# A new order table for a two-layer adaLN kernel on one core: TensorE's signals held back inside groups of indirect transfers

## The reference

```python
h = layernorm(x) * (1 + ca) + sa
x = x + ga * L0_attn(h)    # 16 heads of 8, rope on q and k, softmax over 512 keys
h = layernorm(x) * (1 + cb) + sb
x = x + gb * L0_ffn(h)     # 8 experts, top 2 of each token, silu(h @ w0) * (h @ w1) @ wo
...
h = layernorm(x) * (1 + ca) + sa
x = x + ga * L1_attn(h)    # v, gate = silu(h @ W_hidden); q, k from silu(h @ W_qk)
                           # sim = q.T @ k (256 x 256); out = v * sum(softmax(sim)) * gate @ W_out
h = layernorm(x) * (1 + cb) + sb
x = x + gb * L1_ffn(h)     # expert of a batch: gelu(h @ w1 + b1) @ w2 + b2
```

## Time and profile before

| | before |
|---|---|
| median of 3 runs | 965.92 us (959.76 to 969.08) |
| the profiled execution's own time | 969.92 us |
| its span on the core | 967.7 us |
| mean granted TensorE clock | 0.929 |

### The profile page before, as it was taken

How to read it: one execution, slowest core, us unless ns; L and a number is a source line. 1 busy time by engine, 2 the same in 40 slices (tenths; PEclk the granted TensorE clock), 3 DMA queues, 4 the chain that set the end, 5 groups by cost and what they waited for, 6 DMA issues and landing times. The chain is left out here.

```text
span 967.7 us, 15545 instructions
## 1 busy us (share of the span) xinstructions
PE 803.7 (83%) x4976; PEld 442.4 (46%) x4976; DVE 707.5 (73%) x1415; ACT 576.3 (60%) x907; POOL 469.6 (49%) x609
## 2 busy tenths in 40 slices
PE   4366776899889888999989999988998898688676
PEld 2111122345345534654455545654664466365354
DVE  6688578779878778867778888767686736567664
ACT  2245574757677667765777587567755854433332
POOL 4143125203567546782767376457557653862201
PEclk9669699899999999999899999999999999799787
DMA  6435044353655342295245355552337053110000
GB/s 179 147 106 132 33 81 156 105 116 104 219 139 148 118 137 72 75 273 152 67 110 179 122 156 126 173 172 76 89 102 232 15 176 123 58 38 20 1 23 27
DMA packets 101306, 110.65 MB, mean 114 GB/s; under 512 B 16409, under 2 KB 81049, under 8 KB 99882
## 3 DMA queue, kind: packets, MB, share of 16 engines
q1 hardware_dynamic: 97082, 102.06, 37.3%
q0 software_dynamic: 3584, 7.35, 2.3%
q10 hardware_dynamic: 560, 0.26, 0.1%
HBM read 82.98 MB, written 26.26 MB: 113 GB/s over the span
## 5 line engine op out<-in xcount | busy, mean ns | idle before, releaser
L1754 DVE TENSOR_REDUCE negmax<-scores_for_max 128x2 f32<-128x1024 f32 x252 | 307.6, 1221 | 80.8 <-PE scores_for_max L1050 73.7
L1453 ACT ACTIVATE probs<-scores 128x1024 f32<-128x1024 f32 x256 | 261.7, 1022 | 107.4 <-PE scores L1074 93.5
L1084 PE MATMUL weighted_values<-probs,vaug 128*32 128x512 f32 x1024 | 142.9, 636 | 0.0
L1050 PE MATMUL scores_for_max<-ks,qs 48*128 48x512 bf16 x504 | 103.3, 406 | 42.0 <-DVE negmax L1754 37.0
L1146 PE MATMUL expert_units<-xt,ring 128*128 128x128 f32 x840 | 119.8, 284 | 9.3 <-DVE mu L1938 6.1
L1146 PEld LDWEIGHTS expert_units<-xt,ring 128*128 128x128 f32 x840 | 103.2, 191 | 45.4 <-issue 44.6
L1074 PE MATMUL scores<-qs,ks 51*128 51x512 bf16 x512 | 104.3, 404 | 16.8 <-ACT probs L1453 14.6
L1050 PEld LDWEIGHTS scores_for_max<-ks,qs 48*128 48x128 bf16 x504 | 24.7, 94 | 126.8 <-DVE negmax L1754 96.7
L2217 POOL DMA_INDIRECT xs_d<-xbn,rowpos x56 | 55.0, 983 | 45.0 <-DVE rowpos L1887 30.1
L2228 POOL DMA_INDIRECT y<-ys_d,rowpos x56 | 55.4, 989 | 29.8 <-issue 15.7
L1199 PE MATMUL shared_ab<-ring,mu 128*128 128x128 f32 x420 | 57.8, 283 | 2.5 <-ACT slot_rows L1579 1.1
(11 more groups left out here) (329 smaller groups left out, 1572.0 us busy)
## 6 DMA issues: line engine op xcount, KB each, us to landing
ring<-in_experts SPq DMA_DIRECT2D x113, 384.0 KB, 5.0
slot_rows<-xs_d SPq DMA_DIRECT2D x7, 960.0 KB
parts_d<-parts SPq DMA_DIRECT2D x15, 384.0 KB, 2.7
qs<-parts_d SPq DMA_DIRECT2D x14, 384.0 KB, 6.2
ks<-parts_d SPq DMA_DIRECT2D x14, 384.0 KB, 9.7
ys_d<-slot_rows SPq DMA_DIRECT2D x21, 256.0 KB
w<-in_L_ffn_w SPq DMA_DIRECT2D x16, 256.0 KB, 4.1
parts_d<-parts SPq DMA_DIRECT2D x15, 256.0 KB, 2.9
```

The lines of the kernel that those rows point to most:

```text
L1050: last = nc.tensor.matmul(max_bank(b, g, n)[:, 512 * m:512 * (m + 1)], qs[at, b % 2, p, t * P:(t + 1) * P], ks[at, b % 2, p, :], start=Tru ...
L1084: last = nc.tensor.matmul(pv[32 * j:32 * j + 32, :], vaug[:, kt, PAIRS * (j // 2) + GP * g + j % 2, :], probs[:, kt % 2, j % 2, j // 2, :] ...
L1453: nc.scalar.activation(probs[:, kt % 2, j, :, :].rearrange("p m s -> p (m s)"), se[:, :], ACT.Exp)\
L1754: V.tensor_reduce(negmax[:, g % 2, :, n], max_bank(b, g, n)[:, :].rearrange("p (m s) -> p m s", m=2), AX, ALU.max, negate=True)\
```

## The change

Only `SLOTS` is new. Each step is still done, once, by the same instructions on the same engine, with the same DMAs; what is new is the order on each engine, and with it which user of a shared PSUM bank waits for which. Many steps are empty for some batches (`ldown`, `row` and `upb` do something for batch 7 alone), and their numbers move too, without an effect. Of the steps that do something, 597 of 1231 stand at another place on TensorE, 295 of 688 on ScalarE, 328 of 753 on VectorE, 95 of 301 on GpSimd and 55 of 184 on SyncE. Up to about 157 us the orders are practically the same, and up to about 475 us they differ little. The search went on from the old order; in its picture of the chip TensorE's signals (its semaphore updates) are now held back while GpSimd is inside a group of indirect transfers.

Some lines of the diff:

```diff
-        ("C", "upb"): dict(pe=(1, 2, 3, 4, 5, 6, 7, 11, 12, 13, 14, 15, 16, 17, 1372, 1373)),
+        ("C", "upb"): dict(pe=(1, 2, 4, 12, 16, 17, 18, 20, 21, 22, 23, 24, 25, 26, 1372, 1375)),
...
-        ("C", "row"): dict(pe=(53, 54, 55, 57, 58, 59, 60, 1350)),
+        ("C", "row"): dict(pe=(38, 39, 40, 41, 42, 43, 44, 1347)),
...
-        ("A", "mT"): dict(pe=(157, 179, 200, 221, 244, 268, 298, 312, 339, 382, 402, 436, 460, 508, 544, 560, 607,
-        634, 668, 732, 778, 803, 844, 888, 924, 950, 993, 1050, 1081, 1133, 1177, 1217)),
+        ("A", "mT"): dict(pe=(157, 179, 200, 221, 244, 268, 298, 312, 339, 382, 402, 439, 461, 509, 544, 560, 607,
+        634, 668, 732, 778, 811, 865, 895, 926, 958, 998, 1048, 1085, 1128, 1175, 1200)),
...
-        ("C", "qk"): dict(pe=(534, 546, 687, 698, 840, 852, 992, 1025, 1130, 1139, 1242, 1259, 1325, 1329, 1358,
-        1359)),
-        ("C", "hid"): dict(pe=(556, 562, 581, 586, 713, 719, 734, 740, 867, 873, 891, 896, 1039, 1055, 1060, 1063,
-        1161, 1169, 1185, 1189, 1266, 1269, 1280, 1283, 1341, 1343, 1344, 1346, 1355, 1356, 1360, 1361), act=(249,
...
+        ("C", "qk"): dict(pe=(534, 546, 687, 698, 824, 834, 980, 1017, 1138, 1146, 1241, 1258, 1325, 1330, 1360,
+        1362)),
+        ("C", "hid"): dict(pe=(556, 562, 581, 586, 713, 719, 734, 740, 846, 852, 870, 877, 1029, 1043, 1050, 1057,
+        1171, 1177, 1190, 1193, 1264, 1266, 1279, 1282, 1335, 1344, 1346, 1348, 1355, 1356, 1358, 1359), act=(249,
...
-        ("C", "w2g"): dict(pool=(34, 169, 201, 249, 271, 310, 342, 351)),
+        ("C", "w2g"): dict(pool=(34, 167, 196, 248, 271, 310, 338, 351)),
...
-        ("C", "rstd3"): dict(pool=(129, 170, 213, 257, 298, 312, 347, 352)),
+        ("C", "rstd3"): dict(pool=(129, 170, 204, 250, 298, 312, 347, 352)),
```

More of the change, by code:

```diff
@@ new lines @@
+        ("B", "y"): dict(pe=(261, 388, 523, 659, 844, 963, 1109, 1262)),
+        ("B", "xT"): dict(pe=(275, 413, 549, 686, 869, 1001, 1142, 1281)),
+        ("B", "gate"): dict(pe=(281, 416, 554, 689, 876, 1003, 1145, 1304)),
+        ("B", "rank"): dict(pe=(289, 421, 561, 697, 885, 1007, 1152, 1153)),
+        ("B", "rowT"): dict(pe=(319, 322, 346, 368, 484, 487, 505, 526, 624, 629, 647, 674, 770, 774, 808, 827, 933,
+        937, 956, 977, 1079, 1082, 1099, 1116, 1203, 1206, 1224, 1235, 1236, 1237, 1238, 1239)),
@@ new lines @@
+        ("C", "out"): dict(pe=(594, 595, 746, 747, 886, 888, 1063, 1064, 1197, 1198, 1287, 1288, 1349, 1350, 1373,
+        1374)),
+        ("C", "xT3"): dict(pe=(609, 766, 907, 1074, 1209, 1307, 1351, 1376)),
+        ("C", "up"): dict(pe=(612, 617, 623, 630, 769, 780, 785, 793, 910, 916, 929, 987, 1077, 1084, 1090, 1100,
+        1210, 1215, 1220, 1225, 1309, 1311, 1313, 1314, 1352, 1354, 1357, 1361, 1377, 1378, 1379, 1380), act=(280,
+        285, 288, 294, 370, 378, 383, 391, 450, 456, 462, 498, 542, 548, 555, 564, 616, 621, 626, 632, 676, 678, 680,
@@ L253 @@
-        95, 96, 97, 98, 99, 100, 101, 102, 919, 924, 929, 932, 937, 946, 948, 950)),
-        ("C", "keep"): dict(dve=(45, 46, 47, 103, 104, 105, 106, 958), pool=(113, 151, 193, 236, 266, 305, 337, 341)),
-        ("P", "stats"): dict(dve=(113, 193, 278, 335, 395, 472, 557, 640)),
+        ("P", "split"): dict(act=(35, 38, 44, 53, 62, 76, 121, 131, 190, 206, 279, 317, 363, 384, 483, 495), dve=(181,
+        187, 211, 212, 213, 214, 215, 216, 217, 218, 219, 220, 221, 222, 223, 224), pool=(14, 15, 36, 40, 45, 48, 65,
@@ new lines @@
+        71, 91, 95, 132, 150, 171, 183, 226, 231)),
+        ("P", "split2"): dict(act=(36, 39, 46, 55, 64, 79, 122, 135, 192, 208, 282, 323, 367, 389, 485, 503),
+        dve=(182, 189, 194, 195, 197, 198, 201, 202, 203, 204, 205, 206, 207, 208, 209, 210), pool=(2, 3, 37, 42, 46,
+        51, 67, 73, 92, 100, 133, 153, 173, 185, 228, 234)),
+        ("A", "mrow"): dict(act=(43, 57, 68, 78, 90, 101, 118, 124, 140, 159, 168, 186, 198, 224, 242, 252, 275, 297,
+        315, 354, 377, 401, 426, 442, 460, 478, 504, 527, 549, 576, 595, 607), sp=(61, 63, 66, 68, 70, 74, 77, 80, 82,
@@ new lines @@
+        ("B", "stats"): dict(dve=(332, 399, 472, 554, 651, 728, 807, 885)),
+        ("B", "logits"): dict(dve=(340, 412, 484, 564, 670, 741, 822, 901)),
+        ("B", "top"): dict(dve=(343, 413, 485, 566, 671, 742, 823, 902)),
+        ("B", "place"): dict(dve=(345, 416, 488, 568, 675, 744, 827, 836)),
+        ("B", "weights"): dict(dve=(347, 455, 533, 621, 709, 790, 858, 912)),
+        ("C", "stats"): dict(dve=(456, 536, 622, 712, 794, 860, 913, 949)),
+        ("C", "stats2"): dict(dve=(464, 546, 632, 721, 804, 868, 920, 956)),
@@ new lines @@
+        ("P", "rstd"): dict(pool=(6, 32, 38, 57, 78, 119, 155, 200)),
+        ("A", "vcopy"): dict(pool=(31, 54, 76, 106, 145, 186, 222, 262)),
+        ("C", "w2g"): dict(pool=(34, 167, 196, 248, 271, 310, 338, 351)),
+        ("A", "mparts"): dict(pool=(35, 43, 49, 50, 53, 55, 60, 72, 75, 77, 79, 82, 94, 107, 110, 117, 130, 143, 149,
+        168, 177, 188, 199, 201, 214, 224, 236, 249, 255, 267, 275, 293)),
+        ("B", "rstd"): dict(pool=(56, 80, 114, 152, 198, 233, 266, 309)),
+        ("B", "scatter"): dict(pool=(59, 61, 62, 63, 64, 66, 68, 69, 83, 84, 85, 86, 87, 88, 89, 90, 120, 121, 122,
@@ L323 @@
-        ("B", "fetch"): dict(sp=(75, 76, 85, 89, 92, 95, 106, 109, 112, 115, 126, 132, 134, 138, 149, 153, 158, 161,
-        171, 172, 179, 181, 188, 193, 198, 201, 208, 210, 214, 216, 218, 220)),
+        ("B", "x2"): dict(pool=(108, 144, 184, 223, 261, 301, 331, 332)),
+        ("C", "rstd"): dict(pool=(109, 146, 187, 225, 263, 302, 333, 346)),
+        ("C", "rstd2"): dict(pool=(112, 148, 192, 229, 265, 304, 336, 348)),
+        ("C", "lo"): dict(pool=(116, 154, 194, 235, 269, 306, 340, 341)),
@@ new lines @@
+        ("C", "rstd3"): dict(pool=(129, 170, 204, 250, 298, 312, 347, 352)),
+        ("P", "rope"): dict(sp=(1, 4, 24, 25, 26, 30, 31, 32)),
+        ("P", "second"): dict(sp=(2, 5, 6, 7, 8, 9, 10, 11)),
+        ("P", "raw"): dict(sp=(3, 16, 17, 18, 19, 20, 23, 27)),
+        ("P", "late"): dict(sp=(12, 35, 36, 37, 38, 39, 40, 41)),
+        ("B", "blank"): dict(sp=(13, 14, 21, 22, 28, 29, 33, 34)),
+        ("P", "load"): dict(sp=(15, 43, 58, 72, 84, 103, 124, 155)),
+        ("P", "store"): dict(sp=(42, 44, 62, 64, 67, 69, 79, 81, 98, 100, 119, 130, 142, 145, 168, 175)),
```

255 lines of the change are left out of this document (108 added, 147 removed), and 112 rows, old and new, of the table SLOTS.

## The result

The new order takes 970.4 us in the median of 16 runs (968.59 to 977.91), the old one 966.69 us in 16 runs (959.76 to 973.11). The ratio is 1.0054, with a 95% interval of 1.003 to 1.0078: slower by half a per cent, where 0.25% faster was forecast. The new order's profiled execution took 970.33 us, at its median; that of before took 969.92 us, 3.2 us above the median of its now 16 runs. So the two profiles differ by 0.4 us where the medians differ by 3.7, and single differences between them must be read with that in mind.

The account below looks back on a forecast made before the run. TensorE's own work was taken to bound the middle, chains through VectorE, ScalarE and GpSimd the tail. −2.0 + 1.5 + 0.9 − 1.8 − 1.0 = −2.4 us gave 967.5 profiled, 963.5 us as median; range 951 to 977.

Parts of the forecast that it names:

- middle: 157 to 800 us: same work in another order, few holes to fill; −1 us, ends −8 and +8.
- (a): Around 811 us: hole filled, gate/7 behind out/5, layer 1 of batch 5 and the gathers behind it sooner; −2.0 us.
- (b): Around 879 us: hid0/6, ldown5/7, w07/7 ahead of sim/6, other hid steps behind it, out/6 later; +1.5 us, ends 0 and +3.
- (c): At 920 us: hid1/7 and hid3/7 ahead of qk0/7 and qk1/7, VectorE runs out of work; +0.9 us, ends 0 and +2.
- (d): At 942 us: bias row upb1/7 moves from ahead of out/7 into the hole behind it; −1.8 us.
- The premise: TensorE's signals come late inside groups of indirect transfers; judged unsupported, as the windows' 15.9 us of hole matched their surroundings.
- named risks: In the middle: rstd3/2 waiting ahead of six scatters, up to 5 us; a row DMA behind an expert fetch, some 6 us.
- second risk: In the middle: a row DMA queued behind a fetch of experts, 11 us from mT less 4.6 us cover, some 6 us.
- The first rival: New order fills half of the 15.9 us of holes in the transfer groups: 956.5 us, chance 0.22.
- The second, slower one: Engines stop on steps moved ahead of their data, at rstd3/2 or a row DMA in the middle: 975.5 us, chance 0.23.
- a rule on GpSimd and VectorE against the premise: GpSimd and VectorE lock each other out of a shared port; 2.5 us per meeting by the rule, at most 1.7 traced.

Follow-up runs that it names:

- f2: New order, but the old one between ldown3/7 and xT3/6 (870 to 909 us): 967.0 us against 965.2 before, ratio 1.0011.
- f1: The new order run once more, unchanged: 971.0 us against 965.2 before on the same chip, ratio 1.0066.
- h1: The new order run again, unchanged: 970.9 us against 966.1 before on the same chip, ratio 1.0061.
- f3: New order, but the old one from ldown3/7 to the first pieces of sim/7 (870 to 931 us): 965.3 us against 965.2 before, ratio 1.0003.
- h4: Same kernel as f3, run again: 964.9 us against 966.1 before on the same chip, ratio 1.0004.
- j1: New order, but row/7 behind out/6 on TensorE, lacc7/7 and stats/7 behind hid3/6's step on VectorE: 999.9 us against 1011.4 before, ratio 0.9893.
- e3: Old order, with the new one only behind the first pieces of sim/7: 1002.6 us against 1006.4 before, ratio 0.9965.
- g2: Same kernel as e3, run again on the same chip: 1004.7 us against 1006.2 before, ratio 0.9989.
- j3: Same kernel as e3, run on another chip: 1010.8 us against 1011.4 before, ratio 0.9992.
- e1: Old order, with the new one only between ldown3/7 and xT3/6 (870 to 909 us): 1008.4 us against 1006.4 before, ratio 1.0014.

## Why the prediction was wrong, by its own steps

The forecast was 2.4 us under before, and the new order is 4.8 us over it on open chips (the mean of 3.7, 5.8 and 4.8). Term by term:

| term | forecast | measured | known from |
|---|---|---|---|
| middle | −1.0 | about +1.6 | what the others leave; uncertain by about 3 us |
| (a) | −2.0 | about +0.4 | two profiles |
| (b) | +1.5 | +4.4 (5.2 against the profile of before) | 16 profiles; f2 took back 4.0 |
| (c) | +0.9 | +0.3 | 19 profiles, spread wider than the difference |
| (d) | −1.8 | −1.9 | 19 profiles |

(b) is the largest part of the loss and the one that an experiment shows. It is not the whole miss: with (b) as forecast the kernel would still have been some 2 us slower. (a) won nothing, and the middle may have cost what it was to win. The forecast in absolute time is off by 0.8 us more, because it stood on a median of three runs.

**The premise.** It said that nothing shows a delay that ought to be planned around. For the chip that the profile came from this is right, and two more results on open chips (f1, h1: +0.66 and +0.61%) bear it out. As a statement on the kernel on any chip it is wrong: on two of the four chips of the experiments the delay is there, and the kernel before takes 40 us more there. A profile of one chip could not have told it.

**The middle**, −1 us forecast. The two profiles would give it 4 us of gain (xT/6 at 855.90 against 859.92), but that of before is 3.2 us over its median. Worked out from the loss of 4.8 us on open chips: the stretch at 880 us takes 4.4 of it (52.9 less 48.5, the mean of the eleven old ones), 920 us some 0.3, and the end gives 1.9 back. That leaves 2.0 us for everything ahead of xT/6, of which (a) has some 0.4, with an uncertainty that I put at about 3 us. f3 and h4, which keep only the new middle, (a) and the new end, come out near it: level with before although the end gives 1.9. The sign of this step isn't settled. Its named risks did not happen: rstd3/2 went through between two scatters without a wait, since layer 1 of batch 2 came 17 us sooner, not 12.9. GpSimd's timeline of the new order:

```profile
542.14 0.96 POOL L2217 DMA_INDIRECT xs_d<-xbn,rowpos  x1 [0.30 <-issue]
543.17 0.23 POOL L2102 TENSOR_SCALAR rstd_d<-mv_d 128x4 f32<-128x4 f32 x1
```

TensorE's waits for a row DMA come to 0.2 us. The price of that second risk was read too low: from mT at 156.38 us to `exp` at 169.04 it is 12.7 us and not 11, so that one bad meeting would have been some 8 us.

**(a), −2.0 us forecast, nothing measured.** xT3/5 did come sooner (821.93 us against 828.24, 6.3 us, of which 4.4 were there at the end of sim/5 already), so the 2 us were won on TensorE. The step went wrong in letting the gathers follow. They hang on out/5, which came 4.7 us sooner, 0.3 more than sim/5; the first gather moved from 825.12 to 820.69 and the last piece of x2/6 from 844.53 to 839.66, by 4.4 and 4.9 us, so at most 0.5 more than the shift already there. The up layers reached the same late sum sooner and waited longer: the last hole grew from 3.02 us to 5.63. Behind that hole TensorE was on its lower clock for longer: the 16 matmuls of dn and the 4 behind them take 3.78 and 2.77 us, against 3.49 and 1.88 before. That gave back the half microsecond and more, as xT/6 comes 4.0 us sooner.

```profile
821.93 0.66 PE L1007 MATMUL shared_pc<-ident,xdn 128*128 128x128 f32 x4 [1.86 <-ACT xdn L1437]
...
844.43 1.86 PE L1356 MATMUL shared_pc<-w,kq 128*128 128x128 f32 x7 [5.63 <-DVE kq L2046]
...
820.69 1.07 POOL L2228 DMA_INDIRECT y<-ys_d,rowpos  x1 [0.49 <-issue]
...
839.66 1.29 POOL L682 TENSOR_TENSOR x<-y,x 128x512 f32<-128x512 f32 x1
```

**(b), +1.5 us forecast, 5.2 measured between the two profiles (4.4 against the mean of the old ones): the largest step.** The mechanism and the first half of the sum were right. It put hid2/6 30.6 us behind xT/6; it came 30.9 behind. Wrong was "two steps of 3.07 us" and the 3.7 behind them: 3.5, 4.0 and 4.4 us (together 2.1 us more). I had counted TensorE's work between the steps and put at nothing what that work waits for and the clock. ldown7/7 waits 0.74 us for VectorE's product, which makes hid1/6 0.4 us later. VectorE answers hid1/6 0.9 us later, behind stats/7. hid3/6 runs at the lower clock, 1.63 us for its three pieces against 0.93, so 0.7 us. In j1, without the last two, out/6 comes 1.6 us sooner. Another 1.3 us are the lower clock at out/6 (10.13 us from out/6 to xT3/6 against 8.85); in j1 they stay, so they go with the hole behind hid3/6, now that row/7, ldown7/7 and the rest stand elsewhere. So the clock has 2.0 us of the 5.2. Why it is already down at hid3/6 in the new order, and not in j1, is open.

**(c), +0.9 us forecast, about +0.3 measured.** VectorE's idle gaps before sim/7 came as described (0.38, 0.29 and 0.46 us in the new order), but the time from xT3/6 to sim/7 spreads with either order, from 22.2 to 23.4 us with the old and from 22.8 to 24.1 with the new. The means over 11 and 8 profiles are 23.1 and 23.4 us, so the difference of 0.3 us is smaller than the spread.

**(d), −1.8 us forecast, −1.9 measured.** From sim/7 to the end the old order takes 36.7 us in the mean over 6 profiles, the new one 34.8 over 13 (34.0 to 36.0; the profile of the new order itself is at the upper edge, with 36.0). As whole kernels, e3, g2 and j3 won 3.5, 1.1 and 0.8 us by their ratios, and only the first is clear of no change.

**The rivals and the range.** The result lies inside the range, on the other side of no change. The first rival (the holes in the groups filled) is refuted on the open chips; on the late ones the holes exist and the new middle does fill part of them. The second, slower one had the right sign and the wrong place: TensorE did stop on steps that were moved ahead of their data, but they were ldown7/7 and row/7 at 888 and 892 us (0.74 and 0.70 us), in the tail, and not the two places in the middle. The prediction also set a rule on GpSimd and VectorE against the premise. The row that it took as witness, the product of 2.41 us at 837.13 us, overlaps the last gather (836.75 to 837.69 us) for 0.6 us only and then runs beside an elementwise sum of GpSimd, so it is no good witness for a transfer holding up VectorE. In the profile of the new order the four products of that place take 0.68 to 0.77 us.

## What to carry to other kernels

When a step is put between two links of a chain, cost not only its own work but what it waits for, and what stands on the answering engine just ahead of the answer: here 1.6 us of statistics on VectorE, which the old order did later, held the answer up by 0.96 us. A gain on one engine counts only if the join behind it comes sooner too; find the latest input of the join first. And a plan that hinges on a delay between engines wants a trace from more than one chip: here the change is half a per cent slower on one kind, while five kernels with its middle are 1.0 to 1.7% faster on the other, where the change itself wasn't run.

## What the runs showed of the hardware

On two of the four chips of the experiments, TensorE's signals and SyncE's DMA issues come through late while GpSimd is in a run of indirect transfers: up to 13 us for a signal (e1, done at 758.47 us, taken at 771.58) and 3.35 us instead of 0.99 for one issue (the mean of four). The kernel before takes 40 us more there. In the two groups that were looked at, signals of the first 4 us still came at once. GpSimd's transfers themselves take 0.95 us on both kinds. What makes a chip one or the other is open; it was the same for every kernel run on a chip, and for the one chip that was used twice. And an unchanged stretch of work, like the old order from sim/6 to out/6, takes one of three times (19.8, 20.6 and 22.0 us, in 5, 3 and 3 of 11 profiles), by where TensorE's clock falls in it.
